# Layer-1 attention: dividing the probabilities before the transpose, and one output product for two heads

## The reference

```python
k = jnp.einsum('ihd,bpd->biph', W_K, x)
q = jnp.einsum('ihd,bpd->biph', W_Q, x)
v = jnp.einsum('ihd,bpd->biph', W_V, x)
scores = jnp.einsum('biph,biqh->biqp', k, q)
scores_masked = jnp.tril(scores) - 10000000000.0 * (1.0 - mask)
attn = jax.nn.softmax(scores_masked / np.sqrt(d_head), axis=-1)
z = jnp.einsum('biph,biqp->biqh', v, attn)
z_flat = jnp.transpose(z, (0, 2, 1, 3)).reshape(B, S, -1)
out = jnp.einsum('df,bqf->bqd', W_O, z_flat)
```

## Time and profile before

| what | value |
|---|---|
| runs | 1417.0, 1414.6, 1410.46 us; median 1414.6 |
| the profiled execution's own time | 1415.75 us |
| its span | 1414.0 us |
| TensorE matmul busy | 1295.9 us, 92% of the span |
| TensorE weight load busy | 989.1 us, 70% |
| VectorE busy | 1080.3 us, 76% |
| ScalarE busy | 758.9 us, 54% |
| POOL busy | 344.1 us, 24% |
| mean granted clock of TensorE | 0.968 |

### The profile page before, as it was taken

How to read it: one execution, slowest core, us unless ns; L and a number is a source line. 1 busy time by engine, 2 the same in 40 slices (tenths; PEclk the granted TensorE clock), 3 DMA queues, 4 the chain that set the end, 5 groups by cost and what they waited for, 6 DMA issues and landing times. The chain is left out here.

```text
span 1414.0 us, 26514 instructions
## 1 busy us (share of the span) xinstructions
PE 1295.9 (92%) x8834; PEld 989.1 (70%) x8834; DVE 1080.3 (76%) x3367; ACT 758.9 (54%) x1647; POOL 344.1 (24%) x464
## 2 busy tenths in 40 slices
PE   4379999999999999979987899899999999999996
PEld 2357777777777777655655677778888888878775
DVE  4988888989898988463247876688777788787766
ACT  3316565555555464633332555566666666666663
POOL 4501111111101010100006166433322123333353
PEclk9599999999999999999996999999999999999999
DMA  2000000000000000010000320202221012220012
GB/s 103 1 1 1 1 1 1 1 1 1 1 1 1 1 1 1 1 46 0 0 0 7 86 70 27 68 1 61 61 61 61 23 39 61 60 60 9 9 36 55
DMA packets 39555, 36.21 MB, mean 26 GB/s; under 512 B 2305, under 2 KB 38145, under 8 KB 39169
## 3 DMA queue, kind: packets, MB, share of 16 engines
q1 hardware_dynamic: 37376, 30.36, 7.1%
q0 software_dynamic: 2048, 4.20, 1.0%
HBM read 26.17 MB, written 8.39 MB: 24 GB/s over the span
## 5 line engine op out<-in xcount | busy, mean ns | idle before, releaser
L1099 ACT ACTIVATE pe_<-PS 128x512 f32<-128x512 f32 (+3 forms) x384 | 176.0, 488 | 138.2 <-PE PS L2107 133.8
L1815 DVE CUSTOM_DVE_ANT_0 PS<-PS,mask_row 128x128 f32<-128x128 f32 (+7 forms) x256 | 194.0, 766 | 49.5 <-PE PS L2258 46.2
L1167 ACT ACTIVATE PN<-PS,NM 128x128 f32<-128x128 f32 (+7 forms) x256 | 189.2, 740 | 73.5 <-DVE NM L1815 39.8
L2265 PE MATMUL PS<-ident,PN 128*128 128x128 f32 x1152 | 177.2, 277 | 12.1 <-DVE pe_ L1823 7.4
L2265 PEld LDWEIGHTS PS<-ident,PN 128*128 128x128 f32 x1152 | 136.2, 142 | 50.7 <-issue 32.2
L2257 PE MATMUL PS<-KA,QA 128*128 128x512 f32 (+3 forms) x384 | 158.1, 412 | 14.5 <-issue 6.7
L2087 PE MATMUL PS<-kta,qta 128*128 128x512 f32 (+3 forms) x384 | 148.5, 412 | 11.4 <-DVE tmqs L1489 6.9
L2107 PE MATMUL PS<-qtb,kta 128*128 128x512 f32 (+3 forms) x384 | 132.9, 385 | 0.9 <-ACT pe_ L1099 0.9
L2258 PE MATMUL PS<-KB,QA 128*128 128x512 f32 (+3 forms) x384 | 129.8, 351 | 0.0
L887 POOL TENSOR_SCALAR_AFFINE_SELECT pe_<-pe_ 128x512 f32<-128x512 f32 x64 | 41.1, 642 | 362.6 <-ACT pe_ L1099 362.6
L1489 DVE CUSTOM_DVE_ANT_0 PS<-PS,W 128x128 f32<-128x128 f32 (+3 forms) x256 | 125.0, 495 | 2.7 <-PE PS L2087 1.4
(11 more groups left out here) (309 smaller groups left out, 2921.3 us busy)
## 6 DMA issues: line engine op xcount, KB each, us to landing
W<-w SPq DMA_DIRECT2D x40, 384.0 KB, 4.0
W<-by_expert SPq DMA_DIRECT2D x10, 256.0 KB, 4.7
expert_out<-YS SPq DMA_DIRECT2D x10, 256.0 KB, 2.3
W<-w SPq DMA_DIRECT2D x1, 2508.0 KB, 10.9
by_expert<-WOZ SPq DMA_DIRECT2D x2, 1024.0 KB, 6.8
W<-w SPq DMA_DIRECT2D x1, 1536.0 KB, 6.0
X<-x SPq DMA_DIRECT2D x2, 512.0 KB, 4.9
out<-X SPq DMA_DIRECT2D x2, 512.0 KB, 3.2
```

What stands on the lines that cost most here:

```text
L1099: act.activation(pe_[:, h, n % 2, 0:w], PS[:, 4 + h % 2, 0:w], ACT.Exp, scale=HD0 ** -0.5)\
L1167: act.activation(prob_rows(u, r), scores_of(u), ACT.Exp, bias=NM[:, u:u + 1], scale=-1.0, accum_out=SM[:, r % 2, u:u + 1]).then_inc(score_ ...
L1815: dve.tensor_tensor_reduce(scores_of(u), scores_of(u), mask_row[:, S - w:S], -HD1 ** -0.5, -MASKED, ALU.add, ALU.min, NM[:, u:u + 1]).then ...
L2265: ins = pe.transpose(PS[:, ring_bank[item, r], (j - 4 * k) * P:(j - 4 * k + 1) * P], prob_rows(u, r)[:, j * P:(j + 1) * P], ident[:, :])
```

## The change

- ScalarE or VectorE divides each row of probabilities by its sum before it is transposed. New step rs u on VectorE: the reciprocal of one row sum. New step nm u: PN row u times that reciprocal, in place, on ScalarE (14 rows) or VectorE (rows 3 and 14). T u waits for nm u, not for ex u.
- As the heads are scaled already, w needs one product for each tile, over both heads' 128 partitions, with the plain weights wo. w now covers a whole group (4, 2 and 2 tiles; w0, w4, w6): 8 products a round for 16. x is one plain addition for each group: three for 16 scaled ones and 4 reciprocals.
- WOZ goes. wo is loaded with the gate's weights. The token buffer XGS has its own memory; it is zeroed by POOL and written to the slots by five DMAs. PN has four buffers (`NPROB` = 4).
- The orders of all four engines are new. Among what moves: all q and k copies to RAW are on ScalarE; all z copies are on VectorE; q0 of the next round comes near the end of a round (it was early); POOL makes kh0, qh1, kh1, kl1, then qh0 and kl0 for one round (it was kh0, qh0, kl0, and later kl1 with kh1 and qh1 of the same round before it); the expert part's down product stands in the same slot as its up products, and mt one slot earlier; the sends are 6, 10, 4 and 12 at other places.

```diff
@@ -205,8 +205,8 @@
         QA, KA, KB = (head_parts(n) for n in ("QA", "KA", "KB"))
         RAW = sb("RAW", [P, 2, S])
         VS = sb("VS", [P, B, TB, P])
-        WOZ = sb("WOZ", [P, H1, D])
-        NPROB = 3
+        XGS = sb("XGS", [P, 2, 4, D])
+        NPROB = 4
         PN = sb("PN", [P, NPROB, S])
         PTB = sb("PTB", [P, 8 * 512])
         Z1 = sb("Z1", [P, 2, 512])
...
         GV = wqkv_n[:, 0:2 * P]
-        lo_ = W1_AT["wo"][0]
-        XGS = W1[:, lo_:lo_ + 1024].rearrange("p (m c n) -> p m c n", m=2, c=4)
         lo_ = W1_AT["w11"][0]
         WST = W1[:, lo_:lo_ + 8 * 3 * HID].rearrange("p (j n) -> p j n", j=8)
         YG = [XM, W1[:, lo_:lo_ + NT * D].rearrange("p (t d) -> p t d", t=NT)]
...
@@ -495,22 +492,24 @@
                 steps.append(((kind,) + tuple(int(n) for n in name[len(kind):].split(".")), late))
             return steps
 
-        PE1 = steps1("S0 T14.1' md0' S1 q1+ T13.1' S2 mt0 S3 T15.0' k0+ T14.0' q0+ S4 T15.1' mu1 T1.0 S5 T0.0 pv2' "
-                     "T2.0 S6 T3.0 mu0 S7 k1+ gate0+ T5.0 S8 T4.0 T6.0 v1+ S9 mu2 S10 w6' T7.0 w4' S11 T8.0 T8.1 pv0 "
-                     "T9.1 T9.0 T10.1 S12 gate1 T10.0 mu3 T11.0 S13 v0+ w0 w2 T11.1 S14 T13.0 S15 T12.1 T12.0 pv1")
-        DVE1 = steps1("mx13' x0' tc11.1' x2' mx14' mx15' cm0' ql1 zc1' cm1' mx0 mx1 qr1+ kd1 mx2 gate1 kr0+ mx3 tc15.1' "
-                     "cm2' mh1 mx5 tc0.0 mx4 tc1.0 ql0+ zc2' cm3' cm4' cm5' mx6 mh0 mx7 mx8 tc6.0 kd0+ gate0+ mx9 mh2 "
-                     "x6' cm7' mx10 x4' cm6' mx11 tc9.1 tc9.0 mx12 gate2 mh3")
-        ACT1 = steps1("ex14' tc12.1' tc14.1' ex15' my0' tc13.1' mc0 tc15.0' ex0 gate0 tc14.0' ex1 qr0+ mg1 ex2 ex3 ex4 "
-                     "ex5 tc3.0 tc2.0 mg0 ex6 kr1+ tc5.0 ex7 tc4.0 ex8 vc1+ mg2 ex9 tc7.0 tc8.1 tc8.0 ex10 ex11 tc10.1 "
-                     "zc0 tc10.0 mg3 tc11.0 ex12 vc0+ ex13 tc13.0 tc12.0")
-        POOL1 = steps1("kh1' qh1' send1 kh0 qh0 kl0 kl1' send0")
+        PE1 = steps1("T11.1' mu1 T12.0' mu0 pv1' S0 T12.1' S1 T13.1' mu2 S2 v0 w0' S3 T14.1' T13.0' T14.0' S4 T15.0' "
+                     "S5 T15.1' T0.0 S6 k1+ gate0+ S7 T1.0 T2.0 pv2' T3.0 S8 T4.0 T5.0 q1+ S9 mu3 k0+ S10 T6.0 w4' "
+                     "T7.0 S11 md0 mt0+ T8.1 S12 gate1 T8.0 v1+ S13 pv0 T9.1 T9.0 T11.0 w6' S14 q0+ T10.0 T10.1 S15")
+        DVE1 = steps1("nm14' rs15' mx1 mx0 mx2 gate1 mh2 zc1' x0' rs0 mx3 tc13.0' tc14.0' mx5 rs1 rs2 tc15.1' cm0' cm1' "
+                     "mx6 mx4 rs3 rs6 mx7 nm3 rs5 rs4 rs7 mx8 mx9 mh3 mx10 tc7.0 rs8 kd0+ gate0+ x4' cm2' zc2' cm3' "
+                     "cm4' cm5' cm6' mx11 mx12 gate2 rs11 rs10 rs9 tc8.1 ql1+ tc8.0 rs12 mx13 kd1+ x6' cm7' zc0 mx14 "
+                     "tc10.0 rs13 tc11.1 mx15 ql0+ mh0+ mh1+ rs14")
+        ACT1 = steps1("tc12.1' tc13.1' mg2 ex0 gate0 vc0 nm15' tc14.1' ex1 nm0 ex2 tc15.0' ex3 tc0.0 nm1 nm2 kr1+ ex6 "
+                     "ex4 ex5 nm6 tc2.0 tc1.0 nm4 nm5 tc3.0 ex7 tc4.0 tc5.0 nm7 qr1+ ex8 mg3 ex9 kr0+ tc6.0 ex10 nm8 "
+                     "my0 mc0+ ex11 ex12 vc1+ nm9 nm11 tc9.1 nm10 tc9.0 tc11.0 ex13 qr0+ tc10.1 nm12 ex14 nm13 tc12.0 "
+                     "mg0+ mg1+ ex15")
+        POOL1 = steps1("qh1' kh1' kl1' send1 qh0' kl0' send0 kh0")
 
         MOE_FROM, BATCHES = 4, TILES1 // 4
         ROUTER_STEPS = 2
         MOE = ("mt", "mc", "mu", "mg", "mh", "md", "my")
-        SENDS = {(("send", 0), 2): range(0, 12), (("send", 1), 3): range(12, 16),
-                 (("send", 0), 3): range(16, 28), (("send", 1), 4): range(28, 32)}
+        SENDS = {(("send", 1), 3): range(0, 6), (("send", 0), 3): range(6, 16),
+                 (("send", 1), 4): range(16, 20), (("send", 0), 4): range(20, 32)}
 
         def rounds(steps):
 
...
@@ -740,21 +735,14 @@
 
             sp.wait_ge(s0_dve.sem, s0_dve.at(("zt", 1), TRIPS - 1))
             sp.wait_ge(s0_pe.sem, s0_pe.at(("to", 1), TRIPS - 1))
-            for lo, hi in ((0, W1_AT["wv"][1]), W1_AT["gate"]):
+            for lo, hi in ((0, W1_AT["wv"][1]), (W1_AT["wo"][0], W1_AT["gate"][1])):
                 sp.dma_start(W1[:, lo:hi], w1_in[:, lo:hi]).then_inc(w1_loaded, 16)
 
-            sp.wait_ge(wo_zero, 1)
-            for lo in range(0, TILES1, H1):
-                n = min(H1, TILES1 - lo)
-                sp.dma_start(by_expert[lo * P:(lo + n) * P, :].rearrange("(j p) d -> p j d", p=P), WOZ[:, 0:n, :])\
-                    .then_inc(slots_cleared, 16)
-            sp.wait_ge(slots_cleared, 48)
-            pairs = WOZ[:, :, :].rearrange("p (m h) n -> p h m n", h=2)
-            lo, hi = W1_AT["wo"]
-            for h in range(2):
-                rows = slice(h * HD1, (h + 1) * HD1)
-                sp.dma_start(pairs[rows, h, :, :], w1_in[rows, lo:hi].rearrange("p (m n) -> p m n", n=D))\
-                    .then_inc(wo_loaded, 16)
+            sp.wait_ge(blank, 1)
+            for lo in range(0, TILES1, 8):
+                sp.dma_start(by_expert[lo * P:(lo + 8) * P, :].rearrange("(j p) d -> p j d", p=P),
+                             XGS[:, :, :, :].rearrange("p m c n -> p (m c) n")).then_inc(slots_cleared, 16)
+            sp.wait_ge(slots_cleared, 16 * (TILES1 // 8))
 
             lo = W1_AT["w11"][0]
             experts_in = w1_in[:, lo:lo + 3 * E1 * HID].rearrange("p (a n) -> p a n", a=3)
...
@@ -988,8 +976,8 @@
                     ins.then_inc(low_k, 1)
                 if (item, r) == (("kl", 1), 0):
                     after(pool, ("kl", 1), 0)
-                    pool.memset(WOZ[:, :, :], 0.0).then_inc(wo_zero, 1)
-                    pool.wait_ge(wo_zero, 1)
+                    pool.memset(XGS[:, :, :, :], 0.0).then_inc(blank, 1)
+                    pool.wait_ge(blank, 1)
 
             after(pool, *last)
             pool.wait_ge(y_stored, 16 * BATCHES)
@@ -1166,6 +1154,10 @@
                             after(act, ("T",) + t, r if u >= NPROB else r - 1)
                     act.activation(prob_rows(u, r), scores_of(u), ACT.Exp, bias=NM[:, u:u + 1], scale=-1.0,
                                    accum_out=SM[:, r % 2, u:u + 1]).then_inc(score_exp, 1)
+                elif kind == "nm":
+                    u = item[1]
+                    after(act, ("rs", u), r)
+                    act.activation(prob_rows(u, r), prob_rows(u, r), ACT.Copy, scale=RS[:, u:u + 1]).then_inc(normed_a, 1)
                 elif kind == "tc":
                     _, u, k = item
                     g = GROUP_OF[u // 2]
@@ -1176,9 +1168,7 @@
                 elif kind == "zc":
                     g = item[1]
                     after(act, ("pv", g), r)
-                    for i in PAIRS:
-                        if GROUP_OF[i] == (g + 1) % 3:
-                            after(act, ("w", i), r - 1 if g < 2 else r)
+                    after(act, ("w", GROUPS[(g + 1) % 3][0]), r - 1 if g < 2 else r)
                     dst, src = z_to(g, r)
                     act.activation(dst, src, ACT.Copy).then_inc(z_a, 1)
                 elif kind in ("qr", "kr"):
...
@@ -1776,7 +1766,7 @@
                     held = False
                 elif kind == "cm":
                     for t in (2 * item[1], 2 * item[1] + 1):
-                        after(dve, ("x", t % TB // 2 * 2), ROUNDS - 2 + t // TB)
+                        after(dve, ("x", GROUPS[GROUP_OF[t % TB]][0]), ROUNDS - 2 + t // TB)
                         for k in range(2):
                             dve.wait_ge(fetched[k], 16 * (t + 1))
                         dve.scalar_tensor_tensor(X[:, t, :], YG[t // TB][:, 2 * (t % TB), :], w_two[:, t, 0:1], X[:, t, :],
@@ -1796,6 +1786,7 @@
                     j = item[1]
                     bank = ring_bank[("mu", j), r]
                     after(dve, ("mg", j), r)
+                    after(dve, ("mh", (j - 1) % 4), r if j else r - 1)
                     dve.scalar_tensor_tensor(GV, TH[:, j % 2, :], 1.0, PS[:, bank, 0:2 * P], ALU.add, ALU.mult)\
                         .then_inc(hid_made, 1)
                     after(dve, ("mh", j, "g"), r)
...
@@ -1856,17 +1845,20 @@
                 elif kind == "x":
                     i = item[1]
                     after(dve, ("w", i), r)
-                    dve.reciprocal(RS[:, 2 * i:2 * i + 4], SM[:, r % 2, 2 * i:2 * i + 4]).then_inc(out_added, 1)
-                    after(dve, ("x", i, "r"), r)
                     after(dve, ("x", i), r - 2)
-                    for n in range(4):
-                        h, t = n // 2, i + n % 2
-                        if h:
-                            after(dve, ("x", i, n - 2), r)
-                        xs = X[:, TB * (r % 2) + t, :]
-                        dve.scalar_tensor_tensor(xs, PS[:, ring_bank[("w", i), r], n * D:(n + 1) * D],
-                                                 RS[:, 2 * t + h:2 * t + h + 1], xs, ALU.mult, ALU.add)\
-                            .then_inc(out_added, 1)
+                    n = len(GROUPS[GROUP_OF[i]])
+                    xs = X[:, TB * (r % 2) + i:TB * (r % 2) + i + n, :]
```

(31 more changed lines are left out.)

15 lines of the change are left out of this document (7 added, 8 removed).

## The result

| | before | after |
|---|---|---|
| runs beside each other | 1415.8 us median of 4 (1410.46 to 1418.27) | 1434.63 us median of 4 (1433.9 to 1437.73) |
| span of the profiled execution | 1414.0 us | 1432.7 us |
| mean granted clock | 0.968 | 0.954 |

The changed kernel takes 1.0145 times as long, interval 1.0126 to 1.0164. The forecast was 1400, faster: wrong in direction, and 1434.6 lies outside the range of 1387 to 1419.

The account below looks back on a forecast made before the run. TensorE was taken to bound the MoE rounds (39.97 us, no waits). Round savings less +6.0 lead-in put the last S0 at 1336.3; gathers ending last gave span 1398.5, plus 1.75 profiled: 1400.3, stated as 1400, range 1387 to 1419.

Parts of the forecast that it names:

- expert round: Rounds with MoE work: 39.97 us falls to 38.4, with 38.18 at best from TensorE's removed output products.
- the sends: Six indirect DMAs on POOL between kl1 and qh0; 0.5 us allowed for them in the first round without MoE.
- the lead-in: Stretch before the first S0: POOL makes half 1's operands first and k0's product starts later, +6.0 us (bounds +4 and +8).
- round 0: First round, 43.4 us: paced by the router steps on VectorE, which the change does not shorten; 0, plus or minus 3.
- rounds 1 to 3: Rounds without MoE: 36.0 us taken for each, changes of -4.5, -2.7 and -6.6 us.
- my two signs of being wrong: Forecast called wrong if round 0 grows by more than 3 us, or the scalings take more than 10.3 us a round.
- The 3 us wait before S8: TensorE's wait before a score product in the 42.6 us round; predicted gone, 3 of that round's -6.6 us.
- The tightest hand-off: Next round's q0 product, late in the round, to its S0: 5.2 us of TensorE work against 5.1 us of preparation.
- The scalings: 14 probability-row scalings a round on ScalarE: 9.2 us taken, between 7.7 and an upper bound of 10.3.
- Tail: After the last S0: 32 gathers start 0.8 us behind it, take 53.2 and end last by some 8 us; span 1398.5.
- 3: Rival: waits replace the removed products, as 14 scalings sit on an in-order engine; MoE rounds stay 39.9, total 1414; chance 0.19.
- 4: Rival: ScalarE becomes the bound as scalings wait for reciprocals; 41.4 a round, 1442, or 1430 with half in short rounds; chance 0.13.

Follow-up runs that it names:

- The first-round experiment: Changed kernel with round 0 alone in another operand order (k0 and q0 first on TensorE, ScalarE, POOL; ql1 and kd1 later): 1426.64 us, ratio 1.0072.

## Why the prediction was wrong

- **What failed** was not the price of the work but the order. I wrote that "nothing is surely late, yet several hand-offs have 0.1 to 0.7 us", and took 38.4 for an expert round, 0.5 us for the sends and +6.0 for the lead-in, without laying out mh1, kh0 behind the sends, or the first round's lists on TensorE. Against my last S0 of 1336.3 the measured 1368.4 is 32.1 us late: 6.1 in the lead-in, 3.1 in round 0, 11.1 in rounds 1 to 3 (41.6, 39.9, 38.1 for 36.5, 36.0, 36.0), 11.1 in rounds 4 to 13 and 0.8 in round 14.
- **Lead-in, +6.0 forecast, +12.1 measured.** The steps of POOL that I named as added in front make 6.6 us by themselves (1.3 + 1.3 + 3.05 + 0.95), and I wrote that the k0 product starts later but gave that nothing. TensorE's order had been turned: k1, the gate product and q1 run ahead of k0, so kh0 starts at 757.46 for 751.67 before, 5.8 us later, and with 6.6 that is 12.4. q0, behind v1, is not copied before 765.09 and would by itself keep S0 back to about 768 (an estimate: its cast of 1.44 us and a low part of 1.39 us come behind it). The first-round experiment gave 11.35 of it back.
- **Round 0, 0 forecast with a bound of 3, measured +3.1.** I held that VectorE's router steps pace it. TensorE waits 5.00 us for nm3, which stands behind those steps on VectorE. Without the division the round is 40.2, so the added steps do lengthen it. It was one of my two signs of being wrong.
- **Sends.** I saw that six indirect DMAs stand between kl1 and qh0 and allowed 0.5 us. At the 1.00 us of a gather in the earlier trace rows and the 0.30 idle before it six are 7.8 us; they take 9.9 (842.90 to 852.8), with one wait for a landing among them, and S0 waits 6.19. I had the row for it and did not multiply. Behind that wait the clock is 0.72 over 10 us, which costs 2.6 us more in round 2, a term that I did not have. With the sends moved, rounds 2 and 3 are 36.6 and 36.8, where I said 36.0 for both: the sizes for rounds without experts held there. Round 1 stayed at 41.5 for 36.5, since the sends then delay kh0. The rows show that; no run tests it.
- **Round 3.** The 3 us wait before S8 and the stretch at clock 0.68 are gone as forecast; from 900 to 910 us the clock is 1.00, in the first 10 us of this round here. A wait of 2.61 us for the tokens of the first batch, which I did not have, came instead, so it is -4.5 for the -6.6 I had.
- **Expert rounds, 38.4 forecast, 39.6 measured.** The tightest hand-off was not the one I named (q0 to S0) but its neighbour on VectorE. ql0 lasts 2.40 us there, and mh1 comes behind it and mh0; T12.1' waits 1.00. Without the wait the round is 38.8. The remaining 0.4 over my number is TensorE's own work: the output products fell by 1.87 us, the 1.79 of the earlier trace rows, but the others grew by 0.7 in the new order, where my sum held them fixed. Which neighbour does it is open.
- **ScalarE and VectorE** were sized well: 33.4 and 30.7 us a round (the window's 33.74 and 31.03 times 39.6 / 40) for 34.4 and 32.9. The scalings alone are 10.4 us a round, over my 9.2 and over the 10.3 that I took as a bound and as a sign of being wrong, and still cost no more than 0.1 us in an expert round.
- **Tail.** The mechanism held, that the gathers end last: they start 0.5 us before the last S0 (I had 0.8 behind it), run 57.6 us from the first to the last start for 53.2, and the attention's last product ends 44.5 us behind the last S0, as forecast. The tail was 2.1 us over the forecast (64.3 for 62.2), so 8.8 of its 10.9 us over before were in the sum. The gathers' 4.4 us over my 53.2 lie in three of their 15 intervals, of 4.6 to 5.3 us; the chain took 53.9 to 57.6 us in the runs with these orders, and what makes an interval long is open.
- **Rivals.** 3 had nearly the right number for expert rounds (39.9 for 39.6) with the wrong wait. 4 had the nearest total, but its 1430 is added up wrong: 1400, 30 and half of 12 make 1436. Its mechanism, a full ScalarE, shows in no run. Rivals 3 and 4 took the lead-in and the gathers as forecast, so that 4's nearness in the total is luck; 26 us of loss against before lie at the ends (12.1, 3.1 and 10.9).
